# A selective scan in which the decay is written to SBUF and C gets a second PSUM buffer

## The reference

```python
delta = soft_clamp(jax.nn.softplus(xn @ W_delta + b_delta))
Bp = xn @ W_B
C = xn @ W_C
A = -jnp.exp(A_log)
half_dA = 0.5 * delta[..., None] * A
denom_inv = 1.0 / jnp.maximum(1.0 - half_dA, STAB_EPS)
A_bar = (1.0 + half_dA) * denom_inv
B_bar = jnp.sqrt(delta)[..., None] * Bp[:, :, None, :] * denom_inv
Bx = B_bar * xn[..., None]
def step(h, inp):
    a_t, bx_t, c_t = inp
    h = a_t * h + bx_t
    y_t = jnp.einsum('bdn,bn->bd', h, c_t)
    return (h, y_t)
y = ys + D_skip * xn
```

## Time and profile before

| | |
|---|---|
| median of 3 timed runs | 4926.3 us (4924.91 to 4930.77) |
| the profiled execution's own time | 4889.58 us |
| its span in the trace | 4887.8 us |
| busy share: PE, DVE, ACT, POOL | 90%, 87%, 75%, 32% |
| the four scan stages, first scan to last scan start | 245.8 us each, some 983 us of the span |
| granted TensorE clock, mean | 0.97 of full speed |

### The profile page before, as it was taken

How to read it: one execution, slowest core, us unless ns; L and a number is a source line. 1 busy time by engine, 2 the same in 40 slices (tenths; PEclk the granted TensorE clock), 3 DMA queues, 4 the chain that set the end, 5 groups by cost and what they waited for, 6 DMA issues and landing times. The chain is left out here.

```text
span 4887.8 us, 90715 instructions
## 1 busy us (share of the span) xinstructions
PE 4401.3 (90%) x33000; PEld 1851.8 (38%) x33000; DVE 4271.8 (87%) x5012; ACT 3642.5 (75%) x6131; POOL 1584.3 (32%) x1080
## 2 busy tenths in 40 slices
PE   5778778777876699999899999999999999999998
PEld 3225225224323355566333333333333333333335
DVE  5997998898898366555699999999999999999996
ACT  5766776676674333443599999999999999999993
POOL 0983893893795300000011111221101311131003
PEclk8998998999998899999999999999999999999998
DMA  2502101201201322221111111221112211222116
GB/s 75 172 1 90 49 1 48 91 1 35 87 1 35 130 90 75 71 87 65 38 35 34 42 36 43 52 54 34 36 35 57 55 36 35 53 56 72 24 29 195
DMA packets 371103, 275.37 MB, mean 56 GB/s; under 512 B 235795, under 2 KB 331886, under 8 KB 368814
## 3 DMA queue, kind: packets, MB, share of 16 engines
q1 hardware_dynamic: 330796, 166.29, 13.1%
q0 software_dynamic: 34720, 100.59, 6.4%
q10 hardware_dynamic: 5202, 3.18, 0.2%
HBM read 150.17 MB, written 118.69 MB: 55 GB/s over the span
## 5 line engine op out<-in xcount | busy, mean ns | idle before, releaser
L1784 DVE TENSOR_REDUCE at_mpart<-at_ps 128x1 f32<-128x1024 f32 x2048 | 2377.2, 1220 | 16.0 <-PE at_ps L1684 15.8
L1769 ACT ACTIVATE at_E<-at_ps 128x512 f32<-128x512 f32 x4096 | 2224.6, 596 | 132.9 <-PE at_ps L1693 20.9
L1700 PE MATMUL at_ps<-at_E,at_vst 128*32 128x256 f32 x16400 | 1311.1, 391 | 0.1
L1684 PE MATMUL at_ps<-at_ks,at_qs 48*128 48x512 f16 x4096 | 896.5, 434 | 14.2 <-DVE at_mpart L1784 14.1
L1693 PE MATMUL at_ps<-at_qs,at_ks 50*128 50x512 f16 x4096 | 782.5, 378 | 1.3 <-ACT at_E L1769 0.4
L1563 POOL DMA_INDIRECT at_y<-yd,at_gidx x128 | 132.5, 1035 | 1574.1 <-DVE at_mx L1789 1514.9
L1684 PEld LDWEIGHTS at_ps<-at_ks,at_qs 48*128 48x128 f16 x4096 | 293.5, 140 | 860.5 <-issue 727.3
L887 POOL TENSOR_TENSOR l_work<-l_work 128x1024 f32<-128x1024 f32 x252 | 593.7, 2356 | 34.0 <-issue 0.4
L783 PE MATMUL l_ps<-l_bc,l_sel 96*128 96x512 bf16 x1024 | 319.3, 396 | 246.9 <-DVE l_work L921 124.1
L1700 PEld LDWEIGHTS at_ps<-at_E,at_vst 128*32 128x32 f32 x16400 | 326.3, 108 | 554.1 <-issue 551.0
L819 PE MATMUL l_ps<-l_work,l_ident 128*128 128x512 f32 x1024 | 493.0, 604 | 5.1 <-DVE l_work L921 5.1
(11 more groups left out here) (263 smaller groups left out, 4188.4 us busy)
## 6 DMA issues: line engine op xcount, KB each, us to landing
xd<-l_zero SPq DMA_DIRECT2D x4, 5120.0 KB, 32.9
yd<-at_late POOLq DMA_DIRECT2D x40, 512.0 KB, 3.0
at_late<-xd POOLq DMA_DIRECT2D x38, 512.0 KB, 5.0
at_qs<-qp SPq DMA_DIRECT2D x132, 128.0 KB
at_ks<-kp SPq DMA_DIRECT2D x396, 32.0 KB
at_late<-in_eW SPq DMA_DIRECT2D x8, 1536.0 KB, 8.6
ot<-at_osb SPq DMA_DIRECT2D x516, 17.0 KB
at_qs<-qp SPq DMA_DIRECT2D x132, 64.0 KB
```

Of the source, the lines that this page charges most:

```text
L1684: mm = pe.matmul(ring[n % 2][:, r, :], peak_queries(m, row, buf, i), m.ks[row, buf, bass.ts(kh, BANK)], start=True, stop=True)
L1700: mm = pe.matmul(O[32 * q:32 * q + 32, :], m.vst[:, par, SLOTS_A * kk + sl, :], m.E[:, sl % 4, kk, bass.ts(q, QG)], start=(sl == 0 and kk ...
L1769: act.activation(m.E[:, sl % 4, kk, bass.ts(hf, BANK)], score_bank(t, 4 * sl + 2 * hf + kk), ACT.Exp, scale=scale).then_inc(s.ex, 1)
L1784: dve.tensor_reduce(m.mpart[:, half, job:job + 1], ring[n % 2].rearrange("p a b -> p (a b)"), AX_X, ALU.max).then_inc(s.ring_free, 1)
```

## The change

`decay` writes to SBUF, to the one slot of `m.work` that was free, number 10, in place of the PSUM pair `pdec`; the scan instruction therefore reads both of its streams, decay and bx, from SBUF. The pair that is free becomes a second `pC`: `spread_c(i)` now waits for hc(i-2) instead of hc(i-1), and hc reads `pC[i % 2]`. The decay still has one buffer and still waits for the scan of the unit before. The order of instructions on each engine is the same as before; only operands and the one wait differ.

```diff
-        y, pC, pB, pdec = m.pair[0], m.pair[1], m.pair[2], m.pair[3]
+        y, pB, pC = m.pair[0], m.pair[2], [m.pair[1], m.pair[3]]
+        dec = work(10)
...
                 def spread_c(i):
                     t0, k, n = unit(i)
-                    if i:
-                        pe.wait_ge(s.hc, i)
-                    spread(pC, n + NS, t0).then_inc(s.c_psum, 1)
+                    if i >= 2:
+                        pe.wait_ge(s.hc, i - 1)
+                    spread(pC[i % 2], n + NS, t0).then_inc(s.c_psum, 1)
...
-                    act.activation(flat(pdec), m.lnd[:, k, t0:t0 + HALF], ACT.Tanh, scale=-0.5,
+                    act.activation(dec, m.lnd[:, k, t0:t0 + HALF], ACT.Tanh, scale=-0.5,
                                    bias=m.adec[:, k, n:n + 1]).then_inc(s.decay, 1)
...
-                    dve.tensor_tensor_scan(h[i % 2], flat(pdec), bx[i % 2], m.carry[:, k, n:n + 1] if t0 else 0.0,
+                    dve.tensor_tensor_scan(h[i % 2], dec, bx[i % 2], m.carry[:, k, n:n + 1] if t0 else 0.0,
                                            ALU.mult, ALU.add).then_inc(s.h, 1)
...
-                    dve.tensor_tensor(hc[i % 2], h[i % 2], flat(pC), ALU.mult).then_inc(s.hc, 1)
+                    dve.tensor_tensor(hc[i % 2], h[i % 2], flat(pC[i % 2]), ALU.mult).then_inc(s.hc, 1)
```

## The result

The changed kernel takes 5386.99 us (median of 4 runs, 5382.79 to 5390.59), the kernel before 4925.6 us beside it (4 runs, 4920.98 to 4930.77): a ratio of 1.0933, interval 1.092 to 1.0946, 461 us slower. The profiled execution of the changed kernel took 5390.6 us, with a span of 5388.8.

What follows compares the result with a forecast made beforehand. VectorE and GpSimd, both full and side by side, bound the kernel. 2.22 + 1.40 + 2.13 = 5.75 us a unit; 252 x (5.75 - 3.90) = 466 us more gives 5356, with 36.7 carried over 5392 us; range 5327 to 5511.

Steps and rivals of the forecast that it cites:

- Turns, both ways: In the scan stages, the scan and GpSimd's two instructions exclude each other, each waiting for the other: 5.75 us a unit; chance 0.83.
- the order of turns: In each unit: scan ends, full product 2.22 us, the 592 columns 1.40, then the next scan 2.13.
- The size of a unit: Scan stages: product 2.22, columns 1.40 and scan 2.13 add up to 5.75 us, against 3.90 before.
- the one from the parts: Unit length from handover times in old rows, with a fixed 0.24 us that GpSimd doesn't lose: 5.75 us.
- whole row lengths: High bound of a unit: 2.35 + 1.45 + 2.35 and 0.07 for the signal, 6.22 us; 5511 us in all.
- a loss in proportion: Low bound of a unit: GpSimd loses 81% of the scan's length, as beside L1930; 5.49 us, 5327 in all.
- The median: Whole kernel: timed median lies 36.7 us above the profiled execution; carried over, 5356 becomes 5392 us.
- TensorE on the high side: Scan stages: TensorE idles more in a longer unit; its slow early matmuls take 5.78 us a unit, adding a little.
- one direction only: Scan waits for GpSimd, GpSimd never for a running scan: 4.58 us a unit, 5098 us; chance 0.08 shared with the quick scan.
- the quick scan: Exclusion both ways, but the scan from SBUF takes 1.07 us: 4.69 a unit, 5125 us; chance 0.08 shared with one direction only.
- the scan that doesn't meet GpSimd: Scan's decay stream doesn't meet GpSimd's reads, VectorE keeps 3.89 us a unit: not slower, 4926 us; chance 0.06.

## Why the prediction held

- **What bounds the kernel.** VectorE and GpSimd, both full and side by side: yes. With the overlap gone the kernel lost 460 us; with fewer columns for GpSimd it won back 163 of them, though VectorE had more to do.
- **C's second buffer, 0.** Right. TensorE's wait for L921 ahead of the spread has gone, and a wait for L897 has taken its place (470.7 us), which holds nobody up: a buffer bought time for an engine that had it.
- **Decay into SBUF, 34 ns of ScalarE each, hidden.** Right: 30 ns (1148 against 1118), and ScalarE's wait for the scan grew from 200.9 to 444.0 us.
- **The scan's own length doesn't change.** Right, 2.35 us where GpSimd is idle, 2284 ns beside memsets.
- **Turns, both ways.** Right. Scan rows of 3.51 (3.5 foretold), product rows of 4.17 (4.2), columns at 1.44. The columns are never stretched, as the order of turns said.
- **The size of a unit.** 5.75 foretold, 5.70 measured. The term that was too large is the product, 2.22 for 2.17; the scan was 2.13 for 2.14, the columns 1.40 for 1.39. In all 453 us of scan instead of 466. Of the three readings of the old rows, the one from the parts (5.75) was right; whole row lengths (6.22) and a loss in proportion (5.49) were both off.
- **The median.** I carried 36.7 us from the profiled execution to the median. That gap looks like one between chips: the kernel before had medians from 4894 to 4926 us in the groups, and some 14 us at most between the runs of one. The record doesn't name the first profile's chip, so this is not shown. The sum was good for the difference between two kernels on one chip. That 5392 came so near to 5387 is in part luck: the scans gave 13 us less than foretold, and some 8 us that no term of the sum held lie outside them.
- **TensorE on the high side.** Not borne out in the unit's length. Its matmuls did become longer, but the scans took 358.9 us in each batch, also with one C, where the granted clock was lowest (0.81 to 0.83 in the scans).
- **Rivals.** Fallen: one direction only (L888 is stretched, not only L914), the quick scan (2284 ns from SBUF), the scan that doesn't meet GpSimd. The Trainium skill's rule in "SBUF — State Buffer", section "Who interferes with whom", held in each part that was tried: two VectorE inputs in SBUF collide with a GpSimd instruction that reads, one that only writes is free (592 ns throughout, in the middle of scans), and the later one waits for the first to end. Whole row lengths, taken literally, would have given 6.15 a unit for 5.70.

## What to carry to other kernels

Before an operand of a VectorE instruction is moved from PSUM to SBUF, count its SBUF inputs: at the second one the scan here took turns with each GpSimd instruction that read SBUF, product or copy, and what ran side by side became a sum. A tile in PSUM can be worth its banks for that alone, even when no one waits for the data. Look in the trace of before for any instruction, however small, of the kind that the change will make, and compare its shortest with its median length: a 128x16 product at 174 and 2262 ns showed beforehand the mechanism that then cost 9%.

## What the runs showed of the hardware

A GpSimd copy with one SBUF input is held by a scan just as a product with two is (673 ns alone, 2397 in the median), a memset isn't (592 ns inside scans). In a handover between the two engines less than the row's length passes: behind the columns' end a scan of 1024 takes 2.14 us and not 2.35, behind the scan's end a product takes 2.17 and not 2.36, so turns cost some 0.2 us less than the row lengths say. And the turnovers of the same program differ by up to 6 us each between two executions, three of them together by 10.6 us (462.2 and 451.6), which is 0.2% of the time: as much as one would like to tell apart.
